# A graph-attention kernel on one core: a tile becomes every fourth node of a block of 512

## The reference

```python
h = jnp.maximum(_layernorm(x, axis=-1), 0.0)
h = h @ W
s_src, s_dst = h @ a[:F_out, 0], h @ a[F_out:, 0]
e = leaky_relu(s_src[:, None] + s_dst[None, :], negative_slope=0.2)
e = jnp.where(adj > 0, e, NEG_INF)
out = x + softmax(e, axis=1) @ h
```

## Time and profile before

| | |
|---|---|
| Time, median of 3 runs | 843.11 us (842.23 to 843.27) |
| The profiled execution: time, and span in its trace | 841.73 us, 839.9 us |
| Busy: DVE, POOL, ACT, PE | 599.7, 559.8, 547.4, 545.6 us |
| DMA packets | 75014, 299.21 MB |
| Mean DMA rate over the span | 356 GB/s |

### The profile page before, as it was taken

How to read it: one execution, slowest core, us unless ns; L and a number is a source line. 1 busy time by engine, 2 the same in 40 slices (tenths; PEclk the granted TensorE clock), 3 DMA queues, 4 the chain that set the end, 5 groups by cost and what they waited for, 6 DMA issues and landing times.

```text
span 839.9 us, 8878 instructions
## 1 busy us (share of the span) xinstructions
PE 545.6 (65%) x1847; PEld 237.8 (28%) x1847; DVE 599.7 (71%) x2790; ACT 547.4 (65%) x374; POOL 559.8 (67%) x575
## 2 busy tenths in 40 slices
PE   4757677677676676666776655767677667666231
PEld 3642122233232222322332222323233222223231
DVE  7905457676776778876777768788797676779983
ACT  3969767767676676767676676676767666676000
POOL 3723777776677667676676775777777767767760
PEclk9889655655555666666556667665655665666555
DMA  9999999999999999999999999999999999993110
GB/s 285 419 300 316 398 398 398 400 398 401 402 402 400 403 402 402 403 400 403 401 403 400 401 401 403 398 389 396 393 391 402 392 399 383 391 396 119 31 26 5
DMA packets 75014, 299.21 MB, mean 356 GB/s; under 512 B 14986, under 2 KB 36274, under 8 KB 42192
## 3 DMA queue, kind: packets, MB, share of 16 engines
q1 hardware_dynamic: 49248, 276.84, 83.7%
q0 software_dynamic: 17024, 17.48, 6.7%
q10 hardware_dynamic: 8688, 4.33, 2.8%
HBM read 307.97 MB, written 8.59 MB: 377 GB/s over the span
## 4 chain that ended last, share of the span: by engine, by line
DMA 74%; ACT 11%; DVE 8%; issue 3%; PE 2%; SPq 1%; ACTq 0%; POOLq 0%; DVEq 0%
DMA adj_buf<-in_adj 74%; ACT mask_buf L423 9%; DVE x_all L718 3%; SPq L236 1%; ACT work L388 1%; PE banks L943 1%; PE banks L912 1%; ACT gathered L403 0%; ACT work L398 0%; DVE x_all L714 0%; PE banks L902 0%; DVE rest L578 0%; DVE words L580 0%; DVE words L576 0%; ACTq L415 0%
## 5 line engine op out<-in xcount | busy, mean ns | idle before, releaser
L327 POOL DMA_INDIRECT gathered<-table,index x512 | 510.5, 997 | 217.0 <-issue 171.5
L423 ACT ACTIVATE mask_buf<-adj_buf,minus_half 128x2048 bf16<-128x2048 int32 x256 | 511.4, 2001 | 210.9 <-DMA adj_buf<-in_adj 209.3
L943 PE MATMUL banks<-mask_buf,bit_ident 128*128 128x512 bf16 x1024 | 414.1, 552 | 147.6 <-ACT mask_buf L423 146.8
L943 PEld LDWEIGHTS banks<-mask_buf,bit_ident 128*128 128x128 bf16 x1024 | 105.3, 124 | 369.4 <-ACT mask_buf L423 225.7
L718 DVE SCALAR_TENSOR_TENSOR x_all<-gathered,weight,x_all 128x128 f32<-128x128 f32 x512 | 158.2, 349 | 9.3
L576 DVE MAX8 words<-banks 128x8 f32<-128x512 f32 x64 | 44.5, 696 | 156.3 <-PE banks L943 156.3
L941 PE MATMUL banks<-key_rows,ones_b 3*128 3x512 bf16 x64 | 33.7, 527 | 62.3 <-ACT mask_buf L423 61.8
L982 PE MATMUL banks<-x_all,one_hot 128*128 128x128 f32 x128 | 40.4, 415 | 13.8 <-DVE x_all L718 13.8
L580 DVE MAX8 words<-rest 128x8 f32<-128x512 f32 x64 | 44.5, 695 | 2.2
L311 POOL TENSOR_SCALAR work<-x_all,mv_all,rstd 128x128 f32<-128x128 f32 x32 | 27.0, 855 | 27.5 <-DVE nbias L535 13.8
L578 DVE MATCH_REPLACE8 rest<-words,banks 128x512 f32<-128x512 f32 x64 | 43.6, 681 | 0.0
(11 more groups left out here) (144 smaller groups left out, 487.6 us busy)
## 6 DMA issues: line engine op xcount, KB each, us to landing
adj_buf<-in_adj SPq DMA_DIRECT2D x256, 1024.0 KB, 21.1
gathered<-table,index POOLq DMA_INDIRECT x512, 2.5
table<-gathered ACTq DMA_DIRECT2D x4, 1040.0 KB, 15.7
out<-x_all SPq DMA_DIRECT2D x31, 128.0 KB
x_all<-in_x SPq DMA_DIRECT2D x2, 512.0 KB, 5.2
w_gathered<-table,w_index POOLq DMA_INDIRECT x16, 3.9
out<-x_all SPq DMA_DIRECT2D x2, 64.0 KB
w_ext<-in_L_gnn_W ACTq DMA_DIRECT2D x1, 64.0 KB, 3.3
```

The source lines that it names most:

```text
L327: nc.gpsimd.indirect_dma_start(g_view[buf][:, b, k, :], None, table, bass.IndirectOffsetOnAxis(index[:, buf, b, k:k + 1], 0), bounds_check ...
L423: nc.scalar.activation(mask_buf[:, u], adj_buf[:, u], ACT.Sign, bias=minus_half[:]).then_inc(mask_ready, 1)
L943: ins = mm(bank, bit_ident[:, h * PART_BITS + c], mask_buf[:, u, c * BIT_COLS:(c + 1) * BIT_COLS], start=False, stop=(h == PARTS - 1 and c ...
```

## The change

A tile becomes every fourth node of a block of 512 nodes: partition p of tile 4q+c is node 512q+4p+c. Four nodes that follow each other in memory then lie in one partition, in four tiles that follow each other. The loads of x move runs of 4 x 512 bytes, the table stores runs of 4 x 520 bytes, and the store of a batch (two tiles) runs of 2 x 512 bytes. A unit of the adjacency matrix still gives each partition 8 KB of one row, but its rows are now rows 512q+4p+c: where the rows of neighbouring partitions lay 32 KB apart in DRAM, they now lie 128 KB apart. The bytes moved, the gathers and the work of the compute engines stay. The number that a record carries for its node (`node0`) follows the new order. The rest of the diff is in the fallback branch.

```diff
+        def rows_of(dram, t, tiles):
+
+            q, c = t // FOUR, t % FOUR
+            return dram[q * FOUR * P:(q + 1) * FOUR * P, :].rearrange("(p c) n -> p c n", c=FOUR)[:, c:c + tiles, :]
...
             for k, (lo, hi) in enumerate(STAT_GROUPS):
-                sp.dma_start(x_all[:, lo:hi, :], x[lo * P:hi * P, :].rearrange("(t p) f -> p t f", p=P)
+                sp.dma_start(x_all[:, lo:hi, :].rearrange("p (q c) f -> p q (c f)", c=FOUR), x[lo * P:hi * P, :].rearrange("(q p c) f -> p q (c f)", p=P, c=FOUR)
                              ).then_inc(x_loaded[k], 16)
 
             def load_unit(i, u):
-                sp.dma_start(adj_buf[:, u, :], adj[bass.ds((i * BATCH + u // PARTS) * P, P),
-                                                   u % PARTS * PART:(u % PARTS + 1) * PART]).then_inc(adj_loaded[u], 16)
+                sp.dma_start(adj_buf[:, u, :], rows_of(adj, i * BATCH + u // PARTS, 1)[
+                    :, 0, u % PARTS * PART:(u % PARTS + 1) * PART]).then_inc(adj_loaded[u], 16)
...
                 sp.wait_ge(out_ready, i + 1)
-                sp.dma_start(out[bass.ds(i * (BATCH * P), BATCH * P), :].rearrange("(b p) f -> p b f", p=P),
-                             x_all[:, bass.ds(i * BATCH, BATCH), :]).then_inc(out_stored[group], 16)
+                sp.dma_start(rows_of(out, i * BATCH, BATCH), x_all[:, i * BATCH:(i + 1) * BATCH, :]).then_inc(out_stored[group], 16)
...
-                sp.dma_start(out[t * P:(t + 1) * P, :], x_all[:, t, :]).then_inc(out_stored[group], 16)
+                sp.dma_start(rows_of(out, t, 1), x_all[:, t:t + 1, :]).then_inc(out_stored[group], 16)
...
-            nc.gpsimd.iota(node0[:], [[P, BATCH]], base=0, channel_multiplier=1).then_inc(iotas, 1)
+            nc.gpsimd.iota(node0[:], [[1, BATCH]], base=0, channel_multiplier=FOUR).then_inc(iotas, 1)
...
                 act.wait_ge(rows_ready, (k + 1) * (FOURS // 4))
-                act.dma_start(table[k * QUARTER * P:(k + 1) * QUARTER * P, :].rearrange("(t p) n -> p t n", p=P),
-                              rows_all[:, k * QUARTER:(k + 1) * QUARTER, :]).then_inc(rows_stored[k], 16)
+                act.dma_start(table[k * QUARTER * P:(k + 1) * QUARTER * P, :].rearrange("(q p c) n -> p q (c n)", p=P, c=FOUR),
+                              rows_all[:, k * QUARTER:(k + 1) * QUARTER, :].rearrange("p (q c) n -> p q (c n)", c=FOUR)
+                              ).then_inc(rows_stored[k], 16)
...
-                done.add(v.tensor_scalar(rec[:, ring, :, REC_NODE], node0[:], float(i * BATCH * P), None, ALU.add))
+                done.add(v.tensor_scalar(rec[:, ring, :, REC_NODE], node0[:], float(i // 2 * FOUR * P + i % 2 * BATCH), None, ALU.add))
```

More of the change, by code:

```diff
@@ L176, in gat_kernel @@
         w_m = sb("w_m", [P, 2], f32)
-        cols = sb("cols", [P, 4], f32)
+        cols = sb("cols", [P, 5], f32)
+        s_row, sd_row = cols[:, 3:4], cols[:, 3:5]
         w_flat = w_gathered[:, :, :].rearrange("p k n -> p (k n)")
@@ L283, in _ @@
                     sp.dma_start(x_row, x[bass.ts(t, P), :]).then_inc(dn_x, 16)
+                    sp.dma_start(sd_row, table[bass.ts(t, P), S_COL:ROW]).then_inc(dn_x, 16)
                     with sp.Fori(0, TILES // 4) as j:
@@ L843, in _ @@
                 dve.nop().then_inc(dn_step, 1)
[L845 to L849, removed]
+                with dve.Fori(0, FOURS) as q:
+                    for c in range(FOUR):
+                        dve.wait_ge(dn_bcast, q * FOUR + (c + 1))
+                        v.tensor_scalar(d_diag, ident[:], sd_all[:, q * FOUR + c, 1:2], None, ALU.mult).then_inc(dn_diag, 1)
+                        dve.wait_ge(dn_bcast, q * FOUR + (c + 2))
+                        v.tensor_copy(dense_d[:, bass.ds(q * (FOUR * P), FOUR * P)].rearrange("p (n c) -> p n c", c=FOUR)[:, :, c],
+                                      banks[:, 4, 0:P]).then_inc(dn_row, 1)
                 dve.wait_ge(dn_row, TILES + 1)
@@ L861, in _ @@
                     dve.wait_ge(dn_tr, t * (TILES // 4) + 1)
-                    dense.add(v.tensor_scalar(dense_e, dense_d, sd_all[:, t, 0:1], None, ALU.add))
+                    dve.wait_ge(dn_x, 32 * t + 32)
+                    dense.add(v.tensor_scalar(dense_e, dense_d, s_row, None, ALU.add))
                     dense.add(v.tensor_scalar(dense_m, dense_adj, 0.0, None, ALU.is_gt))
@@ L877, in _ @@
                     dve.wait_ge(dn_sum, t + 1)
-                    dve.wait_ge(dn_x, 16 * t + 16)
                     dve.wait_ge(dn_out, 16 * t + 16)
```

## The result

The changed kernel takes **830.26 us** (median of 4 runs, 829.99 to 830.48) where the kernel before takes 842.78 (842.23 to 843.27). The ratio is 0.9849, with a 95% interval of 0.9835 to 0.9863: 12.5 us faster. The forecast was 831.2 us. Some kernels further down, and the kernel before beside them, took 988 to 1048 us in runs in which VectorE waited 1.2 us and more between dependent instructions over and over, mostly from 90 us on, and of these only the start is read.

A forecast was written before the change was run, and what follows sets the result against it. DMA throughput was taken to bound the kernel, with a start full of DMA work moving few bytes. Gains of 10.3 (restart) and 1.6 us (result stores) took 841.7 to 829.8, plus 1.4 for the median: 831.2 us, range 827 to 842.

The forecast's parts named there:

- The sixth mask: ScalarE's mask in the start that frees a buffer for the next load; start forecast near 56.8 us, before 62.20.
- The stall: ScalarE's 5.39 us without work behind the second table store's 7.78 us issue; forecast to vanish with 512 runs a store.
- The effective restart: Moment from which the DMA engines serve only the remaining 243 adjacency loads; forecast 60.5 us instead of 70.8, gaining 10.3.
- two limits: Bounds on the restart: ScalarE's path at 58.8 us and the DMA work ahead of it at 59.6 us.
- The rate of 2 KB runs: DMA rate for x and table in the start, taken as 345 GB/s between 287 and 410.
- the best case: Low end of the forecast's own range: 841.7 - (12.0 + 3) + 1.4 = 828 us.
- Stores of the results: 31 output stores, 4.06 MB, in 1 KB runs instead of 512 bytes; 1.6 us gained, between 0 and 4.6.
- The distance of the rows: Adjacency loads with rows four times as far apart; taken to cost nothing, each per cent being 6.7 us.
- Gathers some 10 us sooner: GpSimd's first gathers, before at 75.8 us, start some 10 us sooner, changing nothing in the steady stage.
- Rival 1: In the start, larger runs are hardly faster and DMA work holds the restart at 65.8 us: 837.6 us; chance 0.20.
- rival 3: Change ineffective or gain swallowed, restart staying near 70.8 us: 842 to 843 us; chance 0.08, with a small loss.
- rival 2: In the steady stage, wider row distance slows every adjacency load; at 4% it costs 27 us, 858 us; chance 0.15.

The follow-up runs named there:

- all five kernels: The changed kernel and the four with the first, first two, last two or all table stores in 520-byte runs again: 830.26, 831.30, 834.42, 836.17, 838.99 us.
- the experiment for it: Changed kernel with the results in two stores of 512-byte runs for a batch, not one of 1 KB runs: 1013.24 us, ratio 0.9823.

## Why the prediction was right

- *The whole gain, 11.9 us between the profiled executions:* 11.7 measured (841.73 to 829.99 us). The forecast of the median adds 1.4 us, by which the median before lay above its profiled execution; now it lies 0.3 above.
- *The sixth mask at 56.8 us:* 56.76 measured. The stall went as forecast. Its reason as put (the queue holds about 3000 runs) is refuted by the kernel with only the first store short. That it was worth 5.4 us is not shown either: the short stores were put back with 0.60 us of stall or none, and most of the loss came back with them.
- *The effective restart at 60.5 us, 10.3 us gained:* 60.9 by the same reading; 10.6 us gained at the 23rd mask. It came out with two limits close together, as in the working. With the rates of the next point the DMA work ends at 2 + 10.5 + 33.2 + 11.4 = 57.1 us, 1.7 before ScalarE's 58.8, and 1.6 us of idle DMA time are seen. The 2.1 us between 58.8 and 60.9 are for the larger part the last table store (0.51 MB at 42.8 engine-us per MB are 1.4 us).
- *The rate of 2 KB runs, taken as 345 GB/s midway between two bounds:* q10's 1.4% x 828.2 x 16 / 4.33 MB = 42.8 engine-us per MB, 374 GB/s, for the table; before it was 86.9. For x it is 398. The choice was low for both, which cost nothing, since ScalarE decides. Two slips in the sums move nothing either: midway is 348.5, and the best case counts 3 us beside the restart where the bound of the results alone was 4.6.
- *Stores of the results, 1.6 us:* 1.7 us between the 23rd and the last mask, 0.9 to 1.9 by all five kernels, with the distance of the rows in it. The agreement is partly luck, as the bounds were 0 and 4.6 and the experiment for it told nothing.
- *The distance of the rows at nothing:* shown for 32, 128 and 512 KB in loads that have the engines to themselves. The steady stage keeps 399 GB/s, and 21.46 us from issue to landing where it was 21.55.
- *Gathers some 10 us sooner:* the first starts at 70.3 us in place of 75.8, 5.5 us sooner. It costs nothing, as forecast.
- *Rival 1 (runs of 2 KB hardly faster)* is out by the 374 and 398 GB/s; *rival 3* (the gain swallowed) by the traces; *rival 2* by the stretches from 15 to 27 us.
- What the working did not have: the price of a short store depends on what shares the engines with it, from 28 to 91 ns for a packet. The fixed 173 GB/s in the sum was one value out of that range, and the forecast needed it only for the check against before and for the worst case.

## What to carry to other kernels

Find in the start of a kernel the moment from which the bounding stream runs alone, and list the limits ahead of it with their times; a change is worth what the later of them moves, and here they lay less than 2 us apart in the end. Write large tables in long runs: 2 KB in place of 520 bytes was worth 8.3 of the 12.5 us here. Look at the length of a run in DRAM and not at the packets of the trace: 2 KB packets of x moved at 290 or at 398 GB/s, depending on their runs. An issue of more than half a microsecond on an engine that also computes is worth a look, but its idle time is not yet its price: put it back by itself if you can. Before widening a stride to get longer runs elsewhere, measure the strided stream alone: four times and sixteen times were free here, sixty-four times cost a third of the rate. And before you name the engine that limits a stretch, read which one the others wait for, and at what clock it ran.

## What the runs showed of the hardware

- A DMA issue on ScalarE took 0.4 us, but 3.5 to 7.8 us where 1676 to 1733 runs of 520 bytes from the store issued some 10 us before had still to go; ScalarE's later instructions waited behind it. With 841 or fewer left it took 0.38 us.
- Stores to DRAM in 520-byte runs: 28 ns a packet beside adjacency loads, 42 nearly alone, 91 where loads were just starting again beside them.
- Loads of x in packets of 2 KB: 290 GB/s where a packet is four runs of 512 bytes (117 ns), 398 where it is one run (84 ns).
- Adjacency loads of 8 KB runs: 422 to 423 GB/s with rows 32, 128 and 512 KB apart, 272 GB/s with rows 2 MB apart.
- Sixteen projections on TensorE took 3.67 us at a granted clock of 0.50 and 2.23 us at 1.00. Two executions of the same kernel had the low clock in different stretches, 57 to 63 and 48 to 58 us.
